# Cross attention mask products as four 64x64 quarters, with the keys of two heads in four shifted by 64

## The reference

```python
x = x + jnp.tanh(g_xattn[0]) * _L0_xattn_ref(_layernorm(x, axis=-1), ctx_1024, ctx_1024, mask_Bx1xSxS2_bk1, ...)
# in it, with d_k = 8:
scores = jnp.einsum('bhqd,bhkd->bhqk', qh, kh) / jnp.sqrt(jnp.asarray(D_K, jnp.float32))
scores = jnp.where(mask, NEG, scores)
attn = jax.nn.softmax(scores, axis=-1)
out = jnp.einsum('bhqk,bhkd->bhqd', attn, vh)
```

## Time and profile before

| | us |
|---|---|
| median of 3 runs | 5792.77 (5790.32 to 5793.39) |
| the profiled execution, whole | 5784.99 |
| its span | 5783.2 |
| PE busy | 5490.1 (95%) |
| ACT busy | 3995.5 (69%) |
| DVE busy | 3631.9 (63%) |
| POOL busy | 2653.2 (46%) |
| last exponentials of the cross phase | about 1971 |

### The profile page before, as it was taken

How to read it: one execution, slowest core, us unless ns; L and a number is a source line. 1 busy time by engine, 2 the same in 40 slices (tenths; PEclk the granted TensorE clock), 3 DMA queues, 4 the chain that set the end, 5 groups by cost and what they waited for, 6 DMA issues and landing times.

```text
span 5783.2 us, 146589 instructions
## 1 busy us (share of the span) xinstructions
PE 5490.1 (95%) x51848; PEld 3278.6 (57%) x51848; DVE 3631.9 (63%) x8009; ACT 3995.5 (69%) x10790; POOL 2653.2 (46%) x2284
## 2 busy tenths in 40 slices
PE   5999999999999789999999999999999999999997
PEld 2444444444444356666666666666666666666665
DVE  3666776677667456666666666666666666656664
ACT  2555555555555478787887778787888788878885
POOL 2211221112211166656665666666666666665663
PEclk9999999999999899999999999999999999999999
DMA  3232222222332133333333333333333333333332
GB/s 85 61 71 74 57 73 67 74 64 66 74 75 63 54 103 97 100 104 108 97 100 99 108 100 101 94 109 103 102 93 108 104 104 93 97 115 103 93 98 89
DMA packets 144825, 517.35 MB, mean 89 GB/s; under 512 B 29884, under 2 KB 46140, under 8 KB 125676
## 3 DMA queue, kind: packets, MB, share of 16 engines
q1 hardware_dynamic: 142572, 507.58, 31.0%
q10 hardware_dynamic: 1536, 0.40, 0.0%
HBM read 224.98 MB, written 30.68 MB: 44 GB/s over the span
## 4 chain that ended last, share of the span: by engine, by line
PE 44%; ACT 12%; issue 6%; DVE 2%; POOL 1%; DMA 0%; SPq 0%; ACTq 0%; DVEq 0%; POOLq 0%
PE b_qk L1442 9%; PE b_c L1483 6%; PE b_pt L1381 5%; PE b_o L1401 5%; ACT probs L1144 5%; PE b_sc L1369 4%; PE b_nv L1417 3%; PE b_qk L1453 3%; PE b_sc L1360 2%; ACT L1183 2%; ACT L79 2%; PE b_c L1513 2%; PE b_nv L1513 1%; ACT ln_n L1109 1%; PE b_c L1488 1%
## 5 line engine op out<-in xcount | busy, mean ns | idle before, releaser
L436 ACT ACTIVATE eT<-b_e 128x512 f32<-128x512 f32 (+1 forms) x1664 | 903.2, 594 | 871.5 <-PE b_e L754 751.2
L1144 ACT ACTIVATE probs<-b_sc,nb,rq 128x96 f32<-128x96 f32 (+1 forms) x3072 | 1322.5, 449 | 8.7 <-DVE nb L1277 7.5
L509 DVE CUSTOM_DVE_ANT_0 junk<-b_s,mq 128x1024 bf16<-128x1024 f32 (+1 forms) x1024 | 998.9, 990 | 373.3 <-PE b_s L736 359.1
L1068 POOL TENSOR_TENSOR probs<-probs,rsums 128x512 f32<-128x512 f32 (+1 forms) x768 | 717.2, 934 | 666.4 <-DVE rsums L1213 665.9
L1268 DVE TENSOR_REDUCE b_sc<-b_sc 128x4 f32<-128x512 f32 (+1 forms) x768 | 486.1, 633 | 837.6 <-PE b_sc L1369 837.5
L1131 ACT ACTIVATE probsT<-b_pt 128x512 f32<-128x512 f32 x768 | 455.9, 594 | 579.7 <-PE b_pt L1381 579.7
L1442 PE MATMUL b_qk<-xs,weights 128*128 128x256 f32 x3072 | 740.3, 384 | 59.5 <-ACT sq L1158 31.8
L750 PE MATMUL b_e<-mk,identb 128*128 128x512 bf16 (+1 forms) x1664 | 636.7, 383 | 20.6 <-ACT eT L436 19.9
L1144 ACT ACTIVATION_READ_ACCUMULATOR probs<-b_sc,nb,rq 128x1 f32 x3072 | 645.9, 210 | 0.0
L754 PE MATMUL b_e<-q_op,k_op 75*128 75x256 bf16 (+1 forms) x3328 | 639.8, 273 | 0.0
L1442 PEld LDWEIGHTS b_qk<-xs,weights 128*128 128x128 f32 x3072 | 556.4, 191 | 144.9 <-issue 74.5
(11 more groups left out here) (133 smaller groups left out, 8348.8 us busy)
## 6 DMA issues: line engine op xcount, KB each, us to landing
rot_p<-rot_s SPq DMA_DIRECT2D x768, 256.0 KB, 2.4
rkb<-rk_scr SPq DMA_DIRECT2D x192, 512.0 KB, 6.4
k_op<-k_scr SPq DMA_DIRECT2D x192, 300.2 KB
v<-v SPq DMA_DIRECT2D x192, 256.0 KB, 3.6
k_scr<-kp SPq DMA_DIRECT2D x48, 400.2 KB, 3.5
weights<-in_ffn_w SPq DMA_DIRECT2D x27, 512.0 KB, 5.0
ctxT<-in_ctx SPq DMA_DIRECT2D x17, 800.5 KB, 8.7
q_op<-q_scr SPq DMA_DIRECT2D x144, 64.0 KB
```

The source lines that it names most:

```text
L436: nc.scalar.activation(eT[0:n, g % 2, i * 512:(i + 1) * 512], b_e[i][0:n, :], ACT.Exp).then_inc(s["e_ready"], 1)
L509: nc.vector.tensor_tensor_reduce(junk[:, half, 0:n], b_s[u % 2][:, 0:n], mq[:, p, qt, half * 1024:half * 1024 + n], 1.0, LOWEST, ALU.add, ...
L1068: nc.gpsimd.tensor_tensor(pu, pu, rsums[:, u % 2, :].unsqueeze(2).to_broadcast([P, 4, w]), ALU.mult).then_inc(s["pn_ready"], 1)
L1144: last = nc.scalar.activation(probs[:, t, k % 2, 2 * e + h, c0:P], b_sc[:, 512 * e + h * w:512 * e + (h + 1) * w], ACT.Exp, bias=nb[:, k % ...
```

## The change

Three things change in `cross_phase`, and the inputs with them.

- In the 12 full blocks of a group the mask is written by four products of 64x64 (rows 0 to 63 or 64 to 127 of `identb` and `mk`, 512 columns each) in place of two of 128x128: two into the halves of `b_e[0]`, then two into the halves of `b_e[1]`. In `b_e[0]` the row half equals the partition half; in `b_e[1]` they are crossed. All four come first, then the four score products. The waits for ACT stand ahead of the first pair (`b_e[0]` read) and ahead of the second pair (`b_e[1]` read). The last block, of 65 keys, stays as it was.
- Since the halves are crossed, heads 2 and 3 of each group see their keys shifted by 64: block `kt` of these heads is keys 128 kt + 64 to 128 kt + 191. The context, the key tiles, `k_scr` and the mask blocks are longer by 64 keys or one block (the first 64 keys again at the end).
- The values of these heads must be shifted as well. So each of the 13 value products of `bank` "v" becomes two, for the columns of heads 0 and 1 and for those of heads 2 and 3 of every group: the same size of weights (another 128 keys of `ctxT`), 64 columns each.

```diff
+TURNED = DH
+KEXT = KEYS + TURNED
-        ctxT = sb("ctxT", [P, KEYS])
-        kf = sb("kf", [P, KEYS])
-        kp = sb("kp", [P, 3, KEYS], BF16)
+        ctxT = sb("ctxT", [P, KEXT])
+        kf = sb("kf", [P, KEXT])
+        kp = sb("kp", [P, 3, KEXT], BF16)
-        mt8 = sb("mt8", [P, KT, S], U8)
+        mt8 = sb("mt8", [P, KT + 1, S], U8)
-        mk = sb("mk", [P, 2, KT, S], BF16)
+        mk = sb("mk", [P, 2, KT + 1, S], BF16)
...
                         b = nxt[0]
-                        n = min(512, KEYS - 512 * j)
+                        n = min(512, KEXT - 512 * j)
                         pe.wait_ge(s["ctx_in"], count("ctx_in", b, 16))
...
                             n = min(P, KEYS - k0)
-                            last = nc.tensor.matmul(b_p[0:n, t * P:(t + 1) * P], ctxT[:, k0:k0 + n],
-                                                    w_sb[:, XW_V:XW_V + P], start=True, stop=True)
+                            wv = w_sb[:, XW_V:XW_V + P].rearrange("p (g i e) -> p g i e", g=4, i=2)
+                            to = b_p[0:n, t * P:(t + 1) * P].rearrange("p (g i e) -> p g i e", g=4, i=2)
+                            for i2 in range(2):
+                                last = nc.tensor.matmul(to[:, :, i2, :], ctxT[:, k0 + TURNED * i2:k0 + TURNED * i2 + n],
+                                                        wv[:, :, i2, :], start=True, stop=True)
...
                                 pe.wait_ge(s["mrow_in"], count("mrow_in", b, 48 * (q + 1)))
+                            if n == P:
+
+                                pe.wait_ge(s["e_ready"], count("e_ready", b, 2 * g - 1))
+                                for i in range(2):
+                                    if i:
+                                        pe.wait_ge(s["e_ready"], count("e_ready", b, 2 * g))
+                                    for to in range(2):
+                                        frm = (to + i) % 2
+                                        r, ro = slice(frm * DH, (frm + 1) * DH), slice(to * DH, (to + 1) * DH)
+                                        nc.tensor.matmul(b_e[i][ro, :], identb[r, r],
+                                                         mk[r, p, kt + (i and to), :].unsqueeze(1).to_broadcast([DH, 2, S]),
+                                                         start=True, stop=False, skip_group_check=True)
                             for i in range(2):
 
-                                pe.wait_ge(s["e_ready"], count("e_ready", b, 2 * g + i - 1))
-                                nc.tensor.matmul(b_e[i][0:n, :], identb[0:n, 0:n],
-                                                 mk[0:n, p, kt, :].unsqueeze(1).to_broadcast([n, 2, S]),
-                                                 start=True, stop=False, skip_group_check=True)
+                                if n < P:
+                                    pe.wait_ge(s["e_ready"], count("e_ready", b, 2 * g + i - 1))
+                                    nc.tensor.matmul(b_e[i][0:n, :], identb[0:n, 0:n],
+                                                     mk[0:n, p, kt + i, :].unsqueeze(1).to_broadcast([n, 2, S]),
+                                                     start=True, stop=False, skip_group_check=True)
+                                k0 = kt * P + TURNED * i
                                 for j in range(2):
                                     last = nc.tensor.matmul(
-                                        b_e[i][0:n, j * S:(j + 1) * S], k_op[q][0:MROW + 3, 2 * i + j, kt * P:kt * P + n],
+                                        b_e[i][0:n, j * S:(j + 1) * S], k_op[q][0:MROW + 3, 2 * i + j, k0:k0 + n],
                                         q_op[0:MROW + 3, p, 4 * q + 2 * i + j, :], start=False, stop=True,
                                         skip_group_check=True)
```

## The result

The changed kernel takes 6078.5 us (median of 4 runs, 6010.7 to 6146.7) against 5792.4 us before. The ratio is 1.0455, with a 95% interval of 1.0371 to 1.0539, so it is slower by about 4.5%, where 1.3% was forecast; the forecast range ended at 5925. Ratios in this document leave out runs more than 1.5% above the shortest of the same kernel, here the profiled execution, which is the longest of the four with 6146.7 us. By the medians of all runs it is 4.9%.

The account below looks back on a forecast made before the run. PE's stream was taken to bound the cross phase. A row: masks -0.3, values +2.9, keys +0.1, ACT waits +0.8 and +0.9, so +4.4 us; 16 rows 70, plus 5.6 and 1: +77, 5870 us, range 5825 to 5925.

Parts of the forecast that it names:

- What bounds the kernel: Cross phase: as long as PE's stream, PE 98.5 of 100 us at the full clock, a long step 1.97 us.
- The masks: Mask part of a step at PE: quarters save 0.20 us, two more shape changes spend it; -0.3 us a row.
- The value jobs: Value products at PE: 26 more records a row, paced by weight loads at 0.113 us each; +2.9 us a row.
- The waits for ACT: Steps of the cross phase: none under 1.88 us; short steps +0.8, late exponentials after step 9 +0.9 us a row.
- ACT's long copies in group 0 lie beside bank jobs: Group 0 of each row: these copies were taken as covered, so no added wait for ACT was counted there.
- The sum: Whole kernel: +4.4 us a row, 16 rows 70, plus 5.6 and 1, +77 us; 5870 us, 1.3% slower.
- No price for the shape: Rival at the masks: bf16 products change array shape without a gap, a step saves 0.20 us; 5736 us, 6%.
- Turns in a shared bank: Rival at the masks: quarters writing one bank may not overlap, +0.42 us a step; about 6170 us, 5%.
- Bare loads: Rival in the value jobs: 64-column products hide nothing of the next load, 4.9 us a row; 5902 us, 8%.
- What would make it wrong: Closing sign: total wait for ACT several times 30 us, so that the coupling of PE and ACT sets the time.

Follow-up runs that it names:

- b_long: The kernel before with one extra copy of 512 fp32 columns on ACT in group 0, lengthening PE's wait ahead of step 11; 5818 us, ratio 1.0052.
- b_val: The kernel before with each value product split in two of 64 columns, from the same unshifted keys; 5828.9 us, ratio 1.0072.
- a_noval: The changed kernel with the value products whole as before, without the shift of the values; 5898 us, ratio 1.0178.
- a_full: The changed kernel with the unshifted one of each two value products at all 128 columns, so half are whole; 6024.6 us, ratio 1.0327.
- a_pool_full: The changed kernel with POOL issuing the DMAs of the negated maxima and half of the value products at 128 columns; 5830.8 us, ratio 1.0071.

## Why the prediction was wrong, point by point

- **What bounds the kernel.** PE's stream, rightly, and its cost per step by starts. The step that failed stands here: "at the full clock". The whole sum was made at that clock, for a kernel that had a wait of 1 us in each row, and no rival asked what a longer wait and a thinner stream do to the clock. It was in sight: the trace of before has the clock at 0.50 behind the wait of 3.42 us at 126 us, and back at 141 us (the expectation of b_long puts this stretch at 121 to 142; it is 127 to 141). The prediction even said that PE's wait for ACT would grow, and priced it as time only. Missing: 2 to 4 falls of 69 us, 138 to 277 us. The rows of before that show it, the wait from the timeline and then three stretches with columns as in the earlier trace rows:

```profile
126.18 0.39 PE L750 MATMUL b_e<-mk,identb 128*128 128x512 bf16 x1 [3.42 <-ACT eT L436]
...
125.00:130.00 5.00, 3.82 (x19) 1.62 (x20) 0.42 (x1) 3.48 (x5) 1.88 (x1) 0.74 0.00 1
130.00:135.00 5.00, 5.00 (x23) 1.85 (x21) 2.00 (x4) 2.50 (x5) 4.00 (x2) 0.50 0.60 236
140.00:145.00 5.00, 5.00 (x37) 2.18 (x37) 3.16 (x7) 2.42 (x5) 0.67 (x1) 0.89 0.32 71
```

- **The masks.** Right. First quarter to first scores 0.34 (0.33 forecast), shape change 0.10, long step 1.97 (1.96). The saving is spent on the two changes of shape.
- **The value jobs.** Right in mechanism and nearly in size. A job goes from 0.99 to 1.83 us (457.24 to 459.07); 2.5 us a row by b_val and a_noval in place of 2.9.
- **The waits for ACT.** Short steps of 1.91 against the forecast 1.88, the steps of the last row 1.90 apart (2308.10 to 2310.00) against 1.88. "ACT's long copies in group 0 lie beside bank jobs" was right for time at the wait ahead of step 11, which grew from 1.0 to 1.25 where +0.31 was counted, and missed what that wait did. One step of group 0 was taken as covered and was not: from step 0 to step 1 the first scores came 1.31 us apart (454.39 to 455.70), below the 1.88 that the prediction gives as the least, and now come 1.90 apart (535.68 to 537.58): 0.6 us a row.
- **The sum.** A row at the full clock is 122.8 us against 117.7: +5.0, forecast +4.4. Of this the values are 2.5 (2.9), all the rest 2.5 (1.5), so two errors of the sum partly cancel. 5870 us at the full clock.
- **The rivals.** No price for the shape: refuted, 0.10 us between bf16 products. Turns in a shared bank: refuted, the four quarters start within 0.03 us though both row halves write one bank; the restriction that the Trainium skill states in TensorEngine Tiling (Restrictions and Gotchas) does not show here, where the halves are different partitions, and the bank-and-quadrant rule of the Trainium skill's page PSUM — Partial Sum Buffer (PSUM bank collisions raise a hardware error) fits. Bare loads: refuted, the 16 loads of a value job take 1.86 us, 0.11 apart.
- **What would make it wrong.** The last sentence looked in the right place, waits for ACT, but for their sum. Their sum was harmless; one wait of 1.25 us in the wrong place was not: all waits ahead of masks from 140 to 1900 us are 15.2 us, against 14.8 before.

What stays open: why only some of the waits of equal length make the clock fall, and which property of the stream of quarters (their size, the changes of shape around them or the order) keeps it from returning. Nor is it known why value products that are half whole ended seven low stretches in a_full and not the one in a_pool_full. The runs show that both the quarters and the thin value jobs are needed for 160 us, not what the chip counts.

## What to carry to other kernels

When a change makes PE's stream thinner (smaller tiles, shape changes, short products), look for the stream's longest wait before summing: at a granted clock of 1.00 in the profile of before, that wait may be just short of dropping the clock, and the denser stream may be what brings it back. Ask also what keeps the engine that it waits for: here it was in part a third engine. Compare records per stretch and the granted clock, not busy shares. Before packing the array with quarters, count the changes of shape: two of them at 0.10 us ate a saving of 0.20. Moving a DMA issue, and the wait for its data, off the engine that feeds PE was worth 0.67% on the kernel before by itself.

## What the runs showed of the hardware that I had not expected

- The clock fell to the 1.2 GHz level behind 3 of 13 waits of 1.23 to 1.26 us in the changed kernel, behind 12 of 14 waits of 1.44 to 1.47 us in b_long, and behind none of the 28 waits of 0.97 to 1.07 us in the kernel before and b_val. Length alone does not decide: a wait of 1.73 us at 1948 us of the kernel before had no fall behind it.
- A stream whose records leave PE no idle time (100.00 of 100.00 us) stayed at the low level for 164 us. The kernel with 128x128 masks left it within 3 to 14 us, with whole and with split value products.
- Four 64x64 quarters, two row halves in one bank, start within 0.03 us of each other.
